# Attention and mixture-of-experts block on one Trainium2 core: band mask by a matrix product, routing steps spread over other slots, and three moves between queues

## The reference

```
h = layernorm(x) * (1 + ca) + sa                      # ca, sa, ... from silu(c) @ wmod
q, k, v = heads(h @ w_qkv + b_qkv)                     # 16 heads of 16 features
scores = q @ k.T * SCALE + mask                        # mask: 0 where |i - j| <= 64, else -inf
x = x + ga * (softmax(scores) @ v @ w_out + b_out)
h = layernorm(x) * (1 + cb) + sb
s = sigmoid(h @ gate_w.T); sfc = s + gate_bias         # 64 experts in 8 groups of 8
group_scores = sum of the two best of each group; the 4 best groups stay
topk_idx = the 8 best experts of those groups; topk_w = s there / their sum * 2.5
pos = rank of the token among those that chose the expert; kept if pos < 256
y[expert, pos] = (silu(h @ w_gate) * (h @ w_up)) @ w_down
x = x + gb * sum over the 8 experts of topk_w * y
```

## Time and profile before

| | us |
|---|---|
| median of 3 runs | 1123.03 |
| lowest and highest run | 1120.85, 1125.76 |
| the profiled execution, its own time | 1121.81 |
| span of its trace, first to last instruction | 1120.1 |
| bodies 0 to 7 (slot 0 of body 0 to the last scores) | 64.8 to 687 |
| tail and the wait for the last sent rows | 687 to 788 |
| experts and final sum | 788 to 1120 |

### The profile page before, as it was taken

The page is one execution under the profiler, slowest core; times in us unless marked ns, Lnnn a source line. Parts: engine busy times, 40 slices in busy tenths (PEclk is TensorE's granted clock), DMA queues, the critical chain, the costliest instruction groups (busy, mean ns, idle before and its releaser), DMA issues.

```text
span 1120.1 us, 15016 instructions
## 1 busy us (share of the span) xinstructions
PE 755.9 (67%) x4413; PEld 478.6 (43%) x4414; DVE 531.4 (47%) x1966; ACT 532.0 (47%) x1147; POOL 647.9 (58%) x592
## 2 busy tenths in 40 slices
PE   4679687776876876876876767200897878787800
PEld 2234344434444444444434433100675766565700
DVE  4544456855856857857757675430121111121106
ACT  3057676675775764864864774100333333333300
POOL 5104043178477577576676666777376766676760
PEclk9757888798688788788788875555898989798965
DMA  7664658228328338226325211495799987576769
GB/s 285 157 263 129 217 225 242 85 98 246 114 105 241 114 105 229 102 96 180 110 78 153 81 36 50 138 266 142 227 237 213 219 184 149 102 150 111 147 113 393
DMA packets 147357, 182.90 MB, mean 163 GB/s; under 512 B 18825, under 2 KB 127781, under 8 KB 147276
## 3 DMA queue, kind: packets, MB, share of 16 engines
q1 hardware_dynamic: 112812, 126.66, 37.0%
q0 software_dynamic: 30720, 38.03, 17.5%
q10 hardware_dynamic: 3744, 17.25, 3.9%
HBM read 96.58 MB, written 106.21 MB: 181 GB/s over the span
## 4 chain that ended last, share of the span: by engine, by line
DMA 24%; POOL 24%; PE 18%; issue 13%; DVE 10%; ACT 7%; SPq 3%; POOLq 0%; ACTq 0%; DVEq 0%
DMA acc_d<-ys,xg 12%; POOL slots_d L588 8%; POOL acc_d L667 6%; DMA Ks<-parts_d 5%; DMA parts_d<-parts 3%; DVE junk L1188 3%; POOL parts L550 3%; PE outT L957 3%; POOL r L542 3%; PE scores L919 3%; SPq L400 3%; POOL parts L545 3%; PE stageA L893 2%; ACT PT L729 2%; PE scoresT L941 2%
## 5 line engine op out<-in xcount | busy, mean ns | idle before, releaser
L588 POOL DMA_INDIRECT slots_d<-H,dest x256 | 258.1, 1008 | 108.1 <-issue 62.0
L667 POOL DMA_INDIRECT acc_d<-ys,xg x128 | 198.0, 1547 | 102.5 <-ACT ys L836 72.4
L1188 DVE CUSTOM_DVE_ANT_0 junk<-scores,mask 128x256 bf16<-128x256 f32 x512 | 188.1, 420 | 132.1 <-PE scores L919 129.3
L729 ACT ACTIVATE PT<-scoresT 128x512 f32<-128x512 f32 (+1 forms) x320 | 159.7, 499 | 122.0 <-PE scoresT L941 121.4
L720 ACT ACTIVATE scoresT<-mask 128x512 f32<-128x512 bf16 (+1 forms) x320 | 165.0, 516 | 24.3 <-PE scoresT L1072 14.2
L1120 PE MATMUL scoresT<-xgT,wgu 128*128 128x256 f32 x512 | 139.5, 421 | 51.3 <-ACT xgT L824 51.3
L941 PE MATMUL scoresT<-Qs,Ks 98*128 98x256 bf16 (+1 forms) x640 | 128.7, 295 | 64.1 <-ACT scoresT L720 52.0
L919 PE MATMUL scores<-Ks,Qs 96*128 96x256 bf16 x512 | 118.1, 322 | 34.2 <-DMA Ks<-parts_d 27.8
L1120 PEld LDWEIGHTS scoresT<-xgT,wgu 128*128 128x128 f32 x512 | 104.8, 210 | 76.6 <-ACT xgT L824 60.1
L941 PEld LDWEIGHTS scoresT<-Qs,Ks 98*128 98x128 bf16 x640 | 60.9, 112 | 131.0 <-ACT scoresT L720 83.9
L957 PE MATMUL outT<-PT,Va 128*32 128x256 f32 (+1 forms) x1280 | 109.1, 420 | 0.0
(11 more groups left out here) (193 smaller groups left out, 1185.9 us busy)
## 6 DMA issues: line engine op xcount, KB each, us to landing
xg<-slots_d SPq DMA_DIRECT2D x15, 1296.0 KB, 7.8
slots_d<-blank ACTq DMA_DIRECT2D x26, 648.0 KB, 3.4
parts_d<-parts SPq DMA_DIRECT2D x32, 384.0 KB, 2.6
Qs<-parts_d SPq DMA_DIRECT2D x48, 256.0 KB
Ks<-parts_d SPq DMA_DIRECT2D x48, 256.0 KB
wgu<-L_ffn_w_gate_dram SPq DMA_DIRECT2D x64, 128.0 KB, 3.2
wgu<-L_ffn_w_up_dram SPq DMA_DIRECT2D x64, 128.0 KB, 3.2
wd<-L_ffn_w_down_dram SPq DMA_DIRECT2D x64, 128.0 KB, 3.7
```

Of the source, the lines that this page charges most:

```text
L588: pool.indirect_dma_start(out=slots_d[:, :], in_=H2[bt.par][:, t, :], in_offset=None, out_offset=bass.IndirectOffsetOnAxis(ap=dest[bt.par] ...
L667: pool.indirect_dma_start(out=acc_d[n4 % 2][:, :], in_=ys[n4][:, h, :], in_offset=None, out_offset=bass.IndirectOffsetOnAxis(ap=xg[e // 4 ...
L729: sc_.activation(PT[m % NPT][:, :, 0:w], src, ACT.Exp).then_inc(sems["exp"], 1)
L1188: ins = v.tensor_tensor_reduce(out=junk[:, i, :], in0=bS[n % 2][:, i * 2 * P:(i + 1) * 2 * P], in1=mask[:, edge, :], scale=1.0, scalar=TAK ...
```

## The change

Five things are changed.

1. The mask. `seed` is gone from ACT. In `scoresT` PE now first makes a product of the identity (`identb`, bf16) and the mask, 512 columns wide in slots with u = 1, 2, 3 and 256 wide in the others, which starts the bank anew; the two products of the heads are added to it. PE waits for `exp` of two pairs before where it waited for `seed`. The two start products in the banks are gone as well.
2. The routing table. `norm2`, `h2T`, `lg` and `xhat` stand one slot later, `xs` three slots later, and the twelve parts of `c_route` stand in slots 12 to 19 where they stood in 11 to 16. `e_cnt` moves from slot 16 to 19. `e_key` moves from slot 17 of the body to slot 0 of the next one.
3. The table `SEND`: slots 2 to 10 get 12 sends where they had 16, slots 11 to 19 get 20 where they had 16.
4. In POOL's slot, `a_rstd`, `xb` and `c_rstd` stand ahead of the steps of `a_split`.
5. The DMA of the maxima's rows is issued by ACT, right behind its copy `take_mT`, and is gone from SP's list.

```diff
-    xb=(2,), onT=(2, 3), op=(4, 5), x1=(4, 5), x1_store=(10,), xs=(8,), stats2=(5, 5), c_rstd=(6,), xhat=(6,), norm2=(7, 7),
-    h2T=(8, 9), lg=(10,), route=(11, 11, 12, 12, 13, 13, 14, 14, 15, 15, 16, 16), cnt=(16,), key=(17,), zero=(3,),
+    xb=(2,), onT=(2, 3), op=(4, 5), x1=(4, 5), x1_store=(10,), xs=(11,), stats2=(5, 5), c_rstd=(6,), xhat=(7,), norm2=(8, 8),
+    h2T=(9, 10), lg=(11,), route=(12, 13, 13, 13, 14, 15, 16, 17, 18, 18, 19, 19), cnt=(19,), zero=(3,),
...
-SEND = {22: 2, 23: 1, 24: 2, 25: 2, 26: 1, 27: 2, 28: 3, 29: 1, 30: 2, 31: 1, 32: 2, 33: 3, 34: 1, 35: 1, 36: 2, 37: 2,
-        38: 2, 39: 2}
+SEND = {22: 2, 23: 2, 24: 2, 25: 1, 26: 1, 27: 1, 28: 1, 29: 1, 30: 1, 31: 2, 32: 2, 33: 3, 34: 2, 35: 2, 36: 2, 37: 2,
+        38: 3, 39: 2}
...
-                    if u == 3 and (g < QUADS - 1 or nxt):
-                        mrows(*((now, g + 1) if g < QUADS - 1 else (nxt, 0)))
...
-                    for n in at("split", slot) if nxt else []:
-                        a_split(nxt, n)
                     for _ in at("a_rstd", slot) if nxt else []:
                         a_rstd(nxt)
                     for _ in at("xb", slot) if prev else []:
                         c_xb(prev)
                     for _ in at("c_rstd", slot) if prev else []:
                         c_rstd(prev)
+                    for n in at("split", slot) if nxt else []:
+                        a_split(nxt, n)
...
                 sc_.activation(PT[m % NPT][:, :, 0:w], src, ACT.Exp).then_inc(sems["exp"], 1)
-                if m + 2 < 10 * QUADS:
-                    seed(bt, m + 2)
-                elif bt.b < B - 1:
-                    seed(batch(bt.b + 1), m + 2 - 10 * QUADS)
...
                 sc_.activation(MT[:], bT[0:32, 0:P // 2].bitcast(BF16), ACT.Copy).then_inc(sems["mT"], 1)
+                after(act, "mT", bt, g + 1)
+                act.dma_start(Qs[bt.par][MROW:KROWS, HQ * g:HQ * g + HQ, :].rearrange("a h q -> a (h q)"),
+                              MT[:]).then_inc(sems["mrow_ld"], 16)
...
-                after(pe, "seed", bt, m + 1)
+                after(pe, "exp", bt, m - 1)
+
+                half = mask[:, 1, P:2 * P] if u == 0 else mask[:, 1, 0:P] if u == U - 1 else mask[:, 1, :]
+                mm(bST[m % 2][:, 0:2 * (hi - lo)].rearrange("p (h q) -> p h q", h=2), identb[:],
+                   half.unsqueeze(1).to_broadcast([P, 2, hi - lo]), start=True, stop=False, skip_group_check=True)
...
+                    if slot == 0 and now.b >= 2:
+                        e_key(batch(now.b - 2))
...
-                    for _ in at("key", slot) if prev else []:
-                        e_key(prev)
...
+            e_key(batch(B - 2))
             norm_o(last, QUADS - 1)
```

More of the change, by code:

```diff
@@ L61 @@
     lpart=4, vp=3, v=3, Sp=8 * QUADS, smax=2 * 8 * QUADS, m2=2 * QUADS, mTp=QUADS, mT=QUADS, STp=10 * QUADS,
-    exp=10 * QUADS, seed=10 * QUADS, pv=10 * QUADS, oTs=QUADS, oTp=QUADS, rec=QUADS, on=QUADS,
+    exp=10 * QUADS, pv=10 * QUADS, oTs=QUADS, oTp=QUADS, rec=QUADS, on=QUADS,
     onTp=C, onT=C, op=2, t1=2, xb=2, x1=2, xs=1, stats2=T, aggr2=T, rstd2=4, xn2=T, h2=2, h2Tp=C, h2T=C,
@@ L400, in load_stack @@
                     sp.dma_start(dst[n:MROW:len(PAIRS), :, lo:lo + S], src).then_inc(sems["qk_ld"], 16)
[L402 to L405, removed]
             def body(prev, now, nxt):
@@ L439, in _ @@
             sp.dma_start(mod_d[:, 1:3, :], gates[:, 1, :, :]).then_inc(s_mod_st, 16)
-            mrows(first, 0)
             sp.wait_ge(s_mod_st, 48)
@@ L711, in a_p32 @@
                 sc_.activation(parts[:, j % 2, 0, :], p32[j % 2][:], ACT.Copy).then_inc(sems["hpart"], 1)
[L713 to L721, removed]
             def exps(bt, g, u, p):
@@ L804, in _ @@
                 a_p32(batch(0), j)
-            act.wait_ge(s_pe0, 8)
-            for i in range(2):
-                seed(batch(0), i)
             take_mT(batch(0), 0)
@@ L1069, in _ @@
             gate_sums()
-            for i in range(2):
-                mm(bST[i][:, :], identb[:], mask[:, 0:2, :], start=True, stop=True).then_inc(s_pe0, 1)
             pe.wait_ge(s_v0, 9)
```

## The result

| | before | after |
|---|---|---|
| median, us | 1122.42 | 1083.91 |
| lowest and highest run | 1120.85, 1125.76 | 1082.65, 1088.29 |
| profiled execution, us | 1121.81 | 1088.29 |
| its span; mean granted clock | 1120.1; 0.786 | 1085.9; 0.833 |

The ratio is 0.966, with a 95% interval of 0.9625 to 0.9695: 38.5 us less, where 53.6 were forecast. Both medians are of four runs, the profiled one with them. The profiled execution of the changed kernel is the slowest of its four; the other three have spans of 1080.6 to 1080.8.

What follows compares the result with a forecast made beforehand. The string making `Ks` bounds the body, PE beside it: bodies 2 to 6 gain 40 us, body 1 5.6, body 0 3, body 7 and tail 5. Total 53.6 off 1121.8 gives 1068.2, median 1069; range 1044 to 1098.

Steps and rivals of the forecast that it cites:

- the string: The chain making `Ks` for the next batch, taken to set the body: 82.6 us before, 74.6 forecast.
- D: First fill to the next slot 0, DVE busy: 17.1 us before, 17.6 forecast, bounds 16 and 19.
- A: Slot 0 to POOL's `c_xb`: 6.95 us before, 7.7 forecast with `e_key` ahead of the statistics.
- C: Last split's end to first fill (storing parts, loading `Ks`): 12.90 us before, forecast untouched at 12.9.
- B: `c_xb` to the last split's end on POOL: 45.65 us before, 36.4 forecast, bounds 35.3 and 39.5.
- PE beside it: PE's way from slot 0 to slot 14's first fill: 56.3 us (to 60.4) with identity products.
- The four waits: PE's body 5 waits: mask copy 5.30 us, `split_m` 3.86, copy of V 1.90, `Ks` 3.20; gone or melted into the last.
- Level: PE needs 56.3 us to slot 14's first fill, against 57.0 for `Ks`, so PE keeps pace.
- (a): POOL or PE later than reckoned: 4.18 us wait stays in B, D 19; body 79.1, about 1098 us; chance 0.17.
- (b): String shortens more: B 35.3, A 6.9, D 16; body 71.1, 1045 us and a little below; chance 0.13.
- (c): Stall only moves: projections pace splits, `Ks` lands no earlier, PE waits in slot 14; about 1120 us; chance 0.05.
- (d): Slower: PE runs 40 more products a body at the lower clock; body 93, some 1185 us; chance 0.05.

Runs made afterwards that it cites:

- run 3: Changed kernel with the `SEND` table of the kernel before; 1133.9 us, ratio 0.9942 to the kernel before (changed kernel on those chips 0.984).
- run 8: Changed kernel with routing parts 4 to 6 in slot 13 and later parts a slot or so earlier; 1109.94 us, ratio 0.9751 (unedited there 0.984).
- run 10: Changed kernel with `x1`'s store behind the load of `Ks`, routing parts 4 to 6 in slot 13 and the key behind the statistics; 1062.37 us, ratio 0.9449.
- run 6: Changed kernel with the store of `x1` behind the load of `Ks` in SP's list; 1120.44 us, ratio 0.9814 (unedited there 0.984).
- run 7: Changed kernel with the key behind the statistics in DVE's slot 0; 1123.13 us, ratio 0.9852 (unedited there 0.984).
- run 1: Kernel before with only the mask made as a product of the identity; 1132.77 us, ratio 0.9952 to the kernel before.
- run 2: Changed kernel with the mask copied into the banks by ACT again; 1138.27 us, ratio 0.9983 to the kernel before.
- run 12: Changed kernel with the maxima's rows loaded from SP's queue again; 1087.12 us, ratio 0.9676 to the kernel before.
- run 11: Changed kernel with routing, second norm, `xs` and the key in the slots of the kernel before; 1074.88 us, ratio 0.9559.
- run 4: Changed kernel with each identity product made twice in a row; 1129.89 us, ratio 0.9926 (unedited there 0.984).

## Why the prediction was right, and where it was off

Forecast 1069 with a range of 1044 to 1098, measured 1083.9. The direction, the string and its largest term were right; two terms of it were too small, and some 15 us of the forecast gain did not come.

**The string.** Right. Changes on it moved the time the way that the rows said: sends (run 3), D and A (run 8), and D, A and C together (run 10), where the body came to 74.7 us and the time to 1062. Two did not alone: the store of `x1` (run 6) and the key (run 7) moved C and A and left the time as it was, on chips where pauses lie in the bodies. That run 10 lands on the forecast body, 74.6, is partly luck: A, C and D are 0.6 to 0.8 us below their terms and B is 2.1 above.

**B.** Right within 1.0 us: 36.4 forecast, 37.4 measured, the rest being POOL's wait of 2.33 where 1.2 was taken. Run 3 gives back 2.8 to 4.0 us of it.

**A, mis-sized.** 7.7, bounds 6.9 and 8.2; measured 9.0. The step counted only the key's 1.26 us ahead of the statistics. Routing parts 10 and 11, 434.87 to 437.0, stand there too, since slot 19 runs into slot 0 on a DVE that no longer pauses. The change's own table said so. With the key behind the statistics and the parts a slot earlier, A is 7.0. A shorter A is not won whole, though: 1.5 us of it come back as POOL's wait in B (run 10).

**C, mis-sized.** "Untouched: 12.9" was the failed step; it is 15.0, and 15.5 on average in bodies 2 to 6. `xs` moved from slot 8 to 11, out of B, and I counted that as 2.4 us won without asking who waits for `xs`: the store of `x1`, which stands in slot 10 of SP's list ahead of the load of `Ks`. Of the 2.8 us that C has grown on average, 1.3 lie ahead of the issue of the load: that is the order of SP's list. The other 1.5 lie between the issue and the first fill, 11.4 us where it was 9.9. The store used to be issued 2.2 us ahead of the load and now is issued 0.5 us ahead. With the store behind the load both parts shrink, the issue to 2.8 to 3.8 us behind the split and the fill to 9.1 to 9.7 us behind the issue, although the loads of x still follow at once (run 10). So the store has a hand in both. The second part is the less sure one, as it differs between runs of one kernel too (9.6 to 10.3 and 10.1 to 11.3 us in the two traces of the kernel before). That it is the store's traffic beside the load is likely and was not tested by itself.

**D.** 17.6 forecast, 16.7 measured, within the bounds. That DVE has a part in setting D and A is shown by run 8.

**Sum.** Bodies 2 to 6 gave 21.4 us where 40 were forecast: A and C are 3.4 us of each body, B 1.0, D -0.9, 3.5 in all or 17.5 of the 18.6 missing. Body 5 is a mild one; on average over bodies 2 to 6 A is 8.9, B 37.2, C 15.5 and D 16.7, which is 3.7 us over the forecast and makes up the 18.6. Body 1 gave 7.8 (5.6 forecast), body 0 gave 6.0 (3), the start 2.0 (none). Body 7 and the tail gave 2.2 (5); why less was not followed up.

**PE beside it.** Right: 56.3 us forecast to the first fill of slot 14; measured 495.73 - 434.32 - 4.15 = 57.3, with some 6 us of other waits in it. The identity product costs 0.22 and 0.40 us at the two clocks, as bounded. The granted clock rose from 0.81 to 0.86 in body 5, and from 0.83 to 0.95 in body 1. But it hardly rose at the start of the body, where the 9 us of A have 0.56 (0.50 before). "Level" was right as well: run 10 has 1.4 us of wait for `Ks` left in body 3, and POOL's wait in B grows by 1.5 us there once A is shorter.

**The four waits.** Those for the mask and for `M` went as forecast. A wait that the forecast did not have came in, 1.2 to 3.2 us in bodies 2 to 6, for the second norm in slot 9. Which edit took the wait for the mask away was left open, and the traces settle it by elimination. ACT's wait for `c_rstd`, 4.62 us before, is 4.2 with edit 1 alone (run 1). It is gone with edit 1, 3 or 5 undone (runs 2, 3 and 12), and 0.4 us with edit 2 undone (run 11). What all of the latter have is edit 4, `c_rstd` ahead of the splits; it was not undone by itself.

**The routing step.** The forecast left out 1.5 us of DVE for `sfc`, which took 1.97 us beside splits. It takes 0.42 to 0.46 us in every body of the changed kernel, as in the row without splits. But the row of 1.97 was the longest of eight; of the other seven one is 1.82 and none is above 0.66. That the step is stretched by POOL's work beside it shows best in run 3: in body 2 it starts at 248.19, POOL's `xs` runs from 248.66 to 251.01, and the step takes 3.11 us, to 251.30.

**Edit 2.** The forecast gave it nothing for itself but the 2.4 us of `xs`. It is a loss of some 11 us in this form (run 11).

**Edit 5.** Right: nothing on the string (run 12). By the Trainium skill, page "DMA: Bandwidth & Descriptors", section "Issuing engines are not separate DMA queues", moving an issue to another engine saves only issue time; 0.9676 without the move against 0.966 with it agrees.

**The rivals.** (a) came nearest in size, 79.1 for 78.1, but by other terms than it named: the wait in B shrank and D was short. (b) needed A, B and D at their lower bounds; B and A were not. (c) and (d) did not happen; run 4 shows how far (d) was, since doubling the product costs some 10 us.

## What to carry to other kernels

When a step leaves a critical stretch, follow its result as well as its time: whoever waits for it in an in-order DMA list holds everything listed behind it (here 1.3 us a body). Lay the body out along the string that paces it, and fill the gap in which an engine waits for that string's end (DVE's 3.46 us ahead of the first fills) before spreading work over slots where that engine has none. And a wait named after a copy may belong to whatever held the engine that makes the copy.

## What the runs showed of the hardware

With the identity product doubled the granted clock of body 2 was 0.95 where it was 0.81, and PE's busy time did not grow (65.93 and 68.61 us). On two chips the kernel before took 1140 us for 1124, and on one of them the changed kernel took 1123 for 1084. In the traces from those chips ACT, DVE and PE each stand for mostly 2 to 6 us at a time, often together, with no cause in the profile. What holds them there stays open. That the changed kernel loses more by it because it has few waits of its own left for a pause to fall into is a guess; the kernel before was not traced there.
